# Two edge layers of a graph network on one core: TensorE signals behind drains in place of updates on matmuls

## What is computed

```python
h = relu(layernorm(x))                       # before each of the two layers
# layer 0: graph convolution
deg = segment_sum(ones, dst); dinv = rsqrt(deg)
msg = (h @ W)[src] * (dinv[src] * dinv[dst])[:, None]
x = x + relu(segment_sum(msg, dst) + b)
# layer 1: attention over edges; rows = src, cols = dst
q = (h[src] @ Wq.T + bq);  k = (h[dst] @ Wk.T + bk);  v = (h[dst] @ Wv.T + bv)   # each by heads
w = exp(clip(sum over a head of q * k / 4, -10, 10))
out = segment_sum(w * v, src) / (segment_sum(w, src) + 1e-8) + h
x = x + layernorm(out) * gamma + beta
```

## Time and profile before

| what | value |
|---|---|
| median of three runs | 2849.39 us |
| profiled execution | 2854.68 us |
| its span | 2852.4 us |
| TensorE matmuls | 1823.0 us, 64% |
| TensorE weight loads | 1438.6 us, 50% |
| VectorE | 1832.7 us, 64% |
| ScalarE | 1265.2 us, 44% |
| GpSimd | 1532.9 us, 54% |
| mean granted clock of TensorE | 0.798 of full speed |

### The profile page before, as it was taken

The page is one execution under the profiler, slowest core; times in us unless marked ns, Lnnn a source line. Parts: engine busy times, 40 slices in busy tenths (PEclk is TensorE's granted clock), DMA queues, the critical chain, the costliest instruction groups (busy, mean ns, idle before and its releaser), DMA issues. The chain is left out here.

```text
span 2852.4 us, 43311 instructions
## 1 busy us (share of the span) xinstructions
PE 1823.0 (64%) x10081; PEld 1438.6 (50%) x10082; DVE 1832.7 (64%) x4977; ACT 1265.2 (44%) x3328; POOL 1532.9 (54%) x1595
## 2 busy tenths in 40 slices
PE   5324346766677666766786776766777667677672
PEld 4324334444434444443464666665666566666561
DVE  9858785655555654655574666566666666666666
ACT  8524345756556564655563323233333223233333
POOL 0266666666556565565625555545555555555555
PEclk7766667877878788877898878788888888888886
DMA  3211111111111111111107444445444444445453
GB/s 108 60 45 44 44 40 42 42 44 41 42 37 45 39 42 41 38 42 40 41 27 218 123 127 125 122 118 130 124 125 125 121 123 133 121 123 137 121 124 56
DMA packets 227714, 238.31 MB, mean 84 GB/s; under 512 B 32381, under 2 KB 189565, under 8 KB 227557
## 3 DMA queue, kind: packets, MB, share of 16 engines
q0 software_dynamic: 59984, 143.85, 18.7%
q1 hardware_dynamic: 138133, 79.45, 11.0%
q10 hardware_dynamic: 29568, 14.68, 2.1%
HBM read 219.25 MB, written 18.62 MB: 83 GB/s over the span
## 5 line engine op out<-in xcount | busy, mean ns | idle before, releaser
L303 POOL DMA_INDIRECT rows<-y_tab,idx x832 | 795.6, 956 | 566.9 <-issue 304.8
L1382 POOL DMA_INDIRECT x<-kv_tab,kv_idx x648 | 658.6, 1016 | 592.9 <-DVE msg L1434 384.2
L1605 PE MATMUL ps_kv<-kv_s,hot_low 128*128 x1314 | 405.9, 455 | 147.2 <-DVE hot_low L1406 79.9
L782 ACT ACTIVATE sort_v<-sort_t,staged,minus 128x128 f16<-128x128 f16 x914 | 360.6, 480 | 305.6 <-remote 241.8
L874 PE MATMUL ps_sort<-sort_hi,sort_v 128*128 128x496 f16 x1662 | 416.1, 400 | 123.5 <-issue 122.2
L621 DVE TENSOR_SCALAR sort_v<-iota_h,staged 128x128 f16<-128x128 f16 x748 | 243.9, 326 | 315.1 <-remote 266.2
L1592 PE MATMUL ps_m<-msg,x 128*128 128x136 f32 x1728 | 289.7, 319 | 206.9 <-DVE msg L1434 152.6
L832 PE MATMUL ps_sum<-rows,hot 128*128 128x128 f32 x1664 | 275.6, 321 | 216.6 <-issue 102.2
L1605 PEld LDWEIGHTS ps_kv<-kv_s,hot_low 128*128 128x128 f32 x1314 | 282.9, 230 | 199.4 <-issue 161.1
L832 PEld LDWEIGHTS ps_sum<-rows,hot 128*128 128x128 f32 x1664 | 255.3, 233 | 237.6 <-issue 149.5
L1592 PEld LDWEIGHTS ps_m<-msg,x 128*128 128x128 f32 x1728 | 258.2, 222 | 225.6 <-issue 218.1
(11 more groups left out here) (290 smaller groups left out, 2129.6 us busy)
## 6 DMA issues: line engine op xcount, KB each, us to landing
weights<-tile_tab SPq DMA_DIRECT2D x110, 256.0 KB
x<-tile_tab SPq DMA_DIRECT2D x109, 256.0 KB
weights<-tile_tab ACTq DMA_DIRECT2D x56, 256.0 KB
rows<-y_tab,idx POOLq DMA_INDIRECT x832
x<-kv_tab,kv_idx POOLq DMA_INDIRECT x648
kv_tab<-kv_s SPq DMA_DIRECT2D x12, 512.0 KB
x<-x_in SPq DMA_DIRECT2D x1, 3328.0 KB, 13.0
out<-x SPq DMA_DIRECT2D x12, 256.0 KB
```

The source lines that it names most:

```text
L303: pool.indirect_dma_start(out=rows[:, k * SPAN + n, :], out_offset=None, in_=y_tab, in_offset=bass.IndirectOffsetOnAxis(ap=idx[:, k, n:n + ...
L782: last = nc.scalar.activation(to[:, k % 2, m, :], sort_t[:, k % 2, m, :], ACT.Relu, bias=staged[:, v, c:c + 1], scale=minus[:, v, c:c + 1])
L1382: pool.indirect_dma_start(out=rows[:, u, k, :], out_offset=None, in_=kv_tab, in_offset=bass.IndirectOffsetOnAxis(ap=idx[:, u, k:k + 1], ax ...
L1605: last = nc.tensor.matmul(ps_kv[:, k % 2, :], hot_low[:, w, k * P:(k + 1) * P], kv_s[:, ds(low + w, 1), :], start=w == 0, stop=w == WINDOW ...
```

## The change

All places where TensorE attaches an update to a matmul in the two edge layers lose it. In their place TensorE's queue holds a drain, which waits until the array is empty, and the drain carries the update. In the first layer there is one drain for each group of sums (`ps_sum` and `ps_more`) and one for each move. In the second layer there is one drain for each quad, behind `expand`; it raises `q_ready`, and the sequencer then raises `sum_done[u]` and `fill_done` by two increments of its own. So these two signals rise behind `expand` and no longer behind `sums` and `fill`. Ahead of the loop of the second layer each of the two expansions and three fills gets a drain of its own. The order of the matmuls, what each computes and all waits stay as they are. The updates of the other stages stay on their matmuls.

```diff
@@ first layer, sums
                     for n in range(SPAN):
-                        last = nc.tensor.matmul(ps[:, 0:D], hots[:, n, :], rows[:, k * SPAN + n, :],
-                                                start=n == 0, stop=n == SPAN - 1)
-                    last.then_inc(done, 1)
+                        nc.tensor.matmul(ps[:, 0:D], hots[:, n, :], rows[:, k * SPAN + n, :],
+                                         start=n == 0, stop=n == SPAN - 1)
+                    pe.drain(fusable=False).then_inc(done, 1)
@@ first layer, move
-                                    last = nc.tensor.matmul(ps[:, 0:w], values[:, k % 2, m, :], sort_hi[:, k % 2, m, 0:w],
-                                                            start=False, stop=False)
-                            last.then_inc(moved[k], 1)
+                                    nc.tensor.matmul(ps[:, 0:w], values[:, k % 2, m, :], sort_hi[:, k % 2, m, 0:w],
+                                                     start=False, stop=False)
+                            pe.drain(fusable=False).then_inc(moved[k], 1)
@@ second layer, expand
-                    last.then_inc(q_ready[u], 1)
@@ second layer, sums
-                    last.then_inc(sum_done[u], 1)
@@ second layer, fill
-                    last.then_inc(fill_done, 1)
@@ second layer, the program
-                expand(0, 0, begun[0:QUAD])
-                expand(0, 1, begun[QUAD:2 * QUAD])
+                for u in range(2):
+                    expand(0, u, begun[u * QUAD:(u + 1) * QUAD])
+                    pe.drain(fusable=False).then_inc(q_ready[u], 1)
                 for k in range(QUAD - 1):
                     fill(0, k, begun[2 * QUAD + 1 + k])
+                    pe.drain(fusable=False).then_inc(fill_done, 1)
                 with pe.Fori(0, passes_of(mybir.EngineType.PE)) as i:
                     ahead = of_pass(mybir.EngineType.PE, i + 1, slice(0, GROUP + QUAD))
                     for u in range(QUADS):
                         sums(i, u)
                         fill(i if u < 1 else i + 1, (u + 3) % QUADS, ahead[GROUP + u])
                         expand(i if u < 2 else i + 1, (u + 2) % QUADS, ahead[u * QUAD:(u + 1) * QUAD])
+                        pe.drain(fusable=False).then_inc(q_ready[(u + 2) % QUADS], 1)
+                        pe.sem_inc(sum_done[u], 1)
+                        pe.sem_inc(fill_done, 1)
```

More of the change, by code:

```diff
@@ L1580, in expand @@
                     for k in range(QUAD):
-                        last = nc.tensor.matmul(ps_q[u % 2][:, k, :], hotT[:, u % 2, k, :], q[:, ds(buckets[k], 1), :],
-                                                start=True, stop=True)
-                    last.then_inc(q_ready[u], 1)
+                        nc.tensor.matmul(ps_q[u % 2][:, k, :], hotT[:, u % 2, k, :], q[:, ds(buckets[k], 1), :],
+                                         start=True, stop=True)
                 def sums(i, u):
@@ L1591, in sums @@
                     for k in range(QUAD):
-                        last = nc.tensor.matmul(ps_m[u % 2][k // 2][:, k % 2, 0:MSG], hot[:, u, k, :], msg[:, u, k, :],
-                                                start=True, stop=True)
-                    last.then_inc(sum_done[u], 1)
+                        nc.tensor.matmul(ps_m[u % 2][k // 2][:, k % 2, 0:MSG], hot[:, u, k, :], msg[:, u, k, :],
+                                         start=True, stop=True)
                 def fill(i, k, low):
@@ L1604, in fill @@
                     for w in range(WINDOWS):
-                        last = nc.tensor.matmul(ps_kv[:, k % 2, :], hot_low[:, w, k * P:(k + 1) * P], kv_s[:, ds(low + w, 1), :],
-                                                start=w == 0, stop=w == WINDOWS - 1)
-                    last.then_inc(fill_done, 1)
+                        nc.tensor.matmul(ps_kv[:, k % 2, :], hot_low[:, w, k * P:(k + 1) * P], kv_s[:, ds(low + w, 1), :],
+                                         start=w == 0, stop=w == WINDOWS - 1)
                 begun = of_pass(mybir.EngineType.PE, 0, slice(2 * QUAD, GROUP + QUAD))
-                expand(0, 0, begun[0:QUAD])
-                expand(0, 1, begun[QUAD:2 * QUAD])
+                for u in range(2):
+                    expand(0, u, begun[u * QUAD:(u + 1) * QUAD])
+                    pe.drain(fusable=False).then_inc(q_ready[u], 1)
                 for k in range(QUAD - 1):
                     fill(0, k, begun[2 * QUAD + 1 + k])
+                    pe.drain(fusable=False).then_inc(fill_done, 1)
                 with pe.Fori(0, passes_of(mybir.EngineType.PE)) as i:
```

## The result

The changed kernel takes 3176.48 us in the median of four runs (3158.76 to 3182.06), the kernel before 2855.68 on the same chip (2832.88 to 2870.78). The ratio is 1.115, 95% interval 1.110 to 1.121: slower. The forecast was 2690 us.

What follows compares the result with a forecast made beforehand. It took waits for TensorE's signals, held late while GpSimd gathers, as the bound, with no engine near full. 2854.7 + 16 + 16 - 146 - 50 = 2691, given as 2690 us; 8-in-10 range 2450 to 2960 us.

Steps and rivals of the forecast that it cites:

- The reading of the waits: Both layers: while GpSimd gathers, an update attached to a matmul reaches its semaphore late, 6.0 us in the pass read.
- (c): Layer two: prompt signals shorten a pass from 23.0 to 20.3 us, -146 us in all; bounds 0 and -378 us.
- (d): Layer one: prompt signals save 1 us in each run of gathers, -50 us; bounds 0 and -262 us.
- (a): Both layers: a drain by itself costs 0.3 us, with one a pass of layer two on the path, +16 us.
- (b): Layer two: sum_done, moved behind the expansions, delays VectorE by 0.3 us once a pass, +16 us; bounds 0 and 65 us.
- The first rival: Both layers: drains wait as long as updates did and TensorE can't run ahead; 2924 us, up to 3216; chance 0.28.
- just fits: Layer two: a quad started after the held signal ends at 2225.7, its signal being asked for only at 2226.19.
- The crawl: TensorE, after some 120 to 132 matmuls and loads from a gather run's start, executes only 13 in 12.3 us.

## Why the prediction was wrong

**The reading of the waits was right.** TensorE's updates are late under gathers; with runs of 4 the lateness went, as a hold by gathers demands, and with plain loads too. The earlier trace rows reach 4 us into layer two, whose gathers start at 1540.8, but the list up to 1540 has no "remote" either. One count was off: the 52 runs of 16 gathers are 832 divided by 16, and the trace has 36 runs of 12 or more and 29 of 8.

**The step that failed is the premise of (c) and (d): that a drain's signal is prompt while GpSimd gathers.** It took one drain without a gather beside it, 0.1 us behind the last matmul, and passed on to 457 drains, most of them with gathers. In the changed kernel the drains of the two layers end 638 us in sum behind their matmuls. From this the signs of both large terms turned: (c) -146 became +78 (up to +204 in the other rhythm), (d) -50 became +235. Both bounds reached from 0 to a gain; a loss was left to the rival, though the earlier trace rows showed that matmuls without updates were held up as well, and that was evidence on completion. Both signs that the prediction named for being wrong came: a pass over 22 us (23.8 to 27.3), and layer one off by more than 100 us (235).

**(a) was mis-sized too.** 0.3 us a drain, bounds 0 to 0.6, nearly all covered by waiting: where nothing holds the array, a bare drain in layer two cost 0.65 us and the whole change 1.1 us a quad. The row read for the restart (one load, one wake-up) leaves out that everything TensorE had done ahead, operands' loads and whole quads, now starts only behind the drain, and that the granted clock fell from 1.00 to 0.94 there. That layer one pays just 14 us when runs are short shows that (a)'s cover exists there.

**(b) was right in itself**: moved signals alone are 1.001 (0.997 to 1.005). With a drain behind them they are not free (1.025).

**The first rival was right in mechanism and short in size.** Its sign ("drains last over 1 us in a run of gathers") is what the trace shows. Its 224 us for layer one, counted as a most, is near the 235 that layer one lost, but in part by luck: it is 4.3 us in each of 52 runs, and with the 36 long runs that the trace has it would be 155. But its central 2924 took none of it, and half of the drains' 137. Its sentence that in layer two the quad behind a held signal "just fits" fell: the quads' drains end 146 us late in sum, and in the other rhythm, runs of 12, a pass takes 27.3 us. The range ended at 2960, although the rival's own working went to 3216 us; the time stands inside that working, and with 0.28 on the rival the range should have reached it.

**The crawl** was forecast to go on. It went away. Stretches like that of the earlier trace rows, counted as 13 starts of TensorE in over 6.5 us with no gap over 2.6 us, number 25 in the kernel before and none in the changed one. All 25 lie in layer one; the crawl in layer two that (c) put into the pass stands in neither kernel. None are left with the bare drains either, nor in layer one with runs of 8. That the drain keeps TensorE from having so many instructions open would fit, but isn't shown.

**The page's rule.** The Trainium skill, "PSUM — Partial Sum Buffer", section "Engine vs sequencer instructions", says that a drain waits until the engine is fully idle and wants the increment on the matmul. The page says the second for correctness, against an increment on a trailing nop, and allows one on a drain; so it spoke less plainly against this change than the prediction has it. The measurements agree with the first (the drain is as late as the completion, 0.02 us without gathers, 6 us in the rows above). For the second they add the price: no version with its signals on drains was as fast as its counterpart with them on matmuls.

## What to carry to other kernels

In no run here did a drain tell anything sooner than the update on the last matmul, and it takes away the work that ran on beneath a late signal: before trading one for the other, ask what completes late and who makes it late. Where GpSimd gathers in long runs beside a busy TensorE, try to cut the runs, by a wait for the gathers' own landing at a place where GpSimd has slack; here that gave 5%, where the drains took 11 to 16%. The same wait behind every 4 gathers of layer two cost 3.8%, so where and how often matters. And a price read from one instance outside the disturbed stretch is no price inside it, so its bound has to reach to the loss.

## What was not expected of the hardware

- While GpSimd's gathers run, completions of TensorE's instructions are late once some 30 to 60 loads and matmuls have started in the run: 0.02 us before that, 0.5 to 13.5 us in the mean after. Whether the count or the time in the run matters is open. The signals of VectorE, ScalarE and TensorE's sequencer stay at 0.01 us in the median, by the same count. They aren't always held to the end of the run: at 2457.7 one came while gathers went on to 2459.3.
- A pause of GpSimd of some 3 us (its landing wait) lets the held completions go.
- With drains, the same pass of 12 gathers has two rhythms, 22.9 to 25.8 us (medians of four profiles) as 8 and 4, and 26.8 to 27.3 us as one run, and which of them holds differed between runs on different chips (ratio 1.115 and 1.157). What chooses between them is open.
- A drain ends 0.02 us behind the last matmul where nothing is held, but cost 0.65 us with plain loads, where VectorE was busy for 90% of the time, through what can no longer run ahead and perhaps a granted clock of 0.94 in place of 1.00.
